# Weight block sums by accumulating DMAs in DRAM, and six of eight cms chunks multiplied down in pairs by seven products

## What is computed

```python
# L0, L2: V = 512, H = 2048
attn_out = softmax(q @ k.T * V**-0.5) @ v @ Wp + bp          # q, k, v = x @ Wq, x @ Wk, x @ Wv
cms_out  = gelu(attn_out @ cW1 + cb1) @ cW2 + cb2 + one_hot(target_codes)
modifier = gelu(concat([attn_out, cms_out]) @ mW1 + mb1) @ mW2 + mb2
x = clip(x + cms_out + modifier, 0, 1)
# L1, L3: 512 -> 256 -> 512, weights chosen by each batch's role
y = x + gelu(x @ W_down[role] + b_down) @ W_up[role] + b_up
x = layernorm(y) * gamma[role] + beta[role]
```

## Time and profile before

| | |
|---|---|
| median of 3 runs | 2156.77 us (2155.68 to 2158.98) |
| the profiled execution | 2156.44 us, span 2154.8 us |
| PE busy | 2105.6 us, 98%, 9256 matmuls |
| DVE / ACT / POOL busy | 1537.7 / 1042.1 / 598.7 us |
| DMA | 146.41 MB, 125767 packets |

### The profile page before, as it was taken

The page is one execution under the profiler, slowest core; times in us unless marked ns, Lnnn a source line. Parts: engine busy times, 40 slices in busy tenths (PEclk is TensorE's granted clock), DMA queues, the critical chain, the costliest instruction groups (busy, mean ns, idle before and its releaser), DMA issues.

```text
span 2154.8 us, 24846 instructions
## 1 busy us (share of the span) xinstructions
PE 2105.6 (98%) x9256; PEld 1724.7 (80%) x9256; DVE 1537.7 (71%) x1923; ACT 1042.1 (48%) x1527; POOL 598.7 (28%) x620
## 2 busy tenths in 40 slices
PE   8999999999999999999999999999999999999997
PEld 6888887888788887888877888788887888878884
DVE  4366678776867668876776766977686866787676
ACT  5264445454446444544554544444454644454444
POOL 1001136452001113655000111655400011355420
PEclk9999999999999999999999999999999999999999
DMA  8101131212202112221312111321130211311211
GB/s 304 40 10 59 59 88 49 59 48 78 100 20 88 59 59 69 59 59 59 116 41 88 40 59 42 96 59 59 40 127 20 102 46 59 88 50 59 59 59 39
DMA packets 125767, 146.41 MB, mean 68 GB/s; under 512 B 5952, under 2 KB 100160, under 8 KB 123728
## 3 DMA queue, kind: packets, MB, share of 16 engines
q1 hardware_dynamic: 122912, 130.05, 18.9%
q0 software_dynamic: 1504, 8.49, 1.9%
q10 hardware_dynamic: 1232, 6.29, 0.7%
HBM read 123.84 MB, written 12.58 MB: 63 GB/s over the span
## 4 chain that ended last, share of the span: by engine, by line
PE 85%; DVE 10%; ACT 2%; issue 2%; DMA 0%; SPq 0%; ACTq 0%; DVEq 0%
PE bank L615 28%; PE bank L617 28%; PE bank L616 28%; DVE ring L1321 2%; DVE vc L1363 2%; DVE pc L1493 1%; DVE xa L1358 1%; DVE lsum L1695 1%; ACT ring L955 1%; ACT raw L1098 0%; PE bank L923 0%; DVE xs L1700 0%; DVE xs L1653 0%; DVE xs L1685 0%; DVE raw L1439 0%
## 5 line engine op out<-in xcount | busy, mean ns | idle before, releaser
L1321 DVE TENSOR_TENSOR ring<-stage,ring 128x1024 fp32r<-128x1024 f32 (+1 forms) x312 | 363.4, 1176 | 103.8 <-ACT ring L955 103.6
L551 POOL TENSOR_TENSOR stage<-stage 128x256 f32<-128x256 f32 x120 | 106.3, 886 | 1122.1 <-DMA stage<-cms_w 904.5
L615 PE MATMUL bank<-ph_hi,ring 128*128 128x512 f32 x1048 | 410.6, 392 | 5.4 <-issue 2.4
L617 PE MATMUL bank<-ph_hi,ring 128*128 128x512 f32 x1048 | 407.9, 389 | 0.0
L616 PE MATMUL bank<-ph_lo,ring 128*128 128x512 f32 x1048 | 407.9, 389 | 0.0
L615 PE MATMUL bank<-xa,ring 128*128 128x512 f32 x1016 | 396.0, 390 | 2.9 <-DVE xs L1653 2.1
L617 PE MATMUL bank<-xa,ring 128*128 128x512 f32 x1016 | 395.3, 389 | 0.0
L616 PE MATMUL bank<-xa,ring 128*128 128x512 f32 x1016 | 395.3, 389 | 0.0
L955 ACT ACTIVATE ring<-stage 128x1024 fp32r<-128x1024 f32 (+1 forms) x312 | 296.3, 970 | 111.7 <-PE bank L617 78.3
L615 PEld LDWEIGHTS bank<-ph_hi,ring 128*128 128x128 f32 x1048 | 196.7, 188 | 53.7 <-issue 7.2
L617 PEld LDWEIGHTS bank<-ph_hi,ring 128*128 128x128 f32 x1048 | 196.7, 188 | 41.0
(11 more groups left out here) (159 smaller groups left out, 3139.6 us busy)
## 6 DMA issues: line engine op xcount, KB each, us to landing
stage<-mod_w SPq DMA_DIRECT2D x128, 256.0 KB, 3.4
stage<-cms_w SPq DMA_DIRECT2D x36, 512.0 KB, 3.6
stage<-mod_w SPq DMA_DIRECT2D x32, 512.0 KB, 4.9
stage<-cms_w SPq DMA_DIRECT2D x56, 256.0 KB, 4.3
fold_staging<-fold_w SPq DMA_DIRECT2D x16, 512.0 KB, 5.2
stage<-folded SPq DMA_DIRECT2D x16, 512.0 KB, 4.3
xs<-pc POOLq DMA_DIRECT2D x8, 1024.0 KB, 8.3
stage<-ada_w SPq DMA_DIRECT2D x16, 512.0 KB, 3.6
```

The source lines that it names most:

```text
L551: pool.tensor_tensor(part(S1), part(S2), part(A22), ALU.add).then_inc(sums_ready, 1)
L615: pe.matmul(dst, lh, rh, start=start and n == 0, stop=False, skip_group_check=not start)
L617: done = pe.matmul(dst, ll, rh, start=False, stop=n == last, skip_group_check=not start)
L1321: dve.tensor_tensor(ring_part(key, 1), staged(key), f32(ring_part(key, 0)), ALU.subtract).then_inc(w_lo, 1)
```

## The change

1. **Sums in DRAM.** New DRAM tensors `ready_w` and `ready_pair` hold each piece as seven blocks. SyncE copies the piece's blocks into them, seven DMAs a piece in DRAM (`prepare`); GpSimd adds with accumulating DMAs in rows of 8 KB, three once the copies are there (`sum_once`) and two once those are (`sum_twice`). Then `load_ready` brings all seven blocks to the staging buffer (896 KB, rows of 1 KB; 2 KB for a pair). The layer's 33 pieces (30, and three double ones) are cut in batches: for layer 0 one of three and one of five at the start, then two a slot in slots 0 to 7 and three from slot 8; for layer 1 two and four. Batch `n` is copied in SyncE's turn of slot `n + 1`, summed once in GpSimd's slot `n + 2` and twice in slot `n + 3`. Layer 0 is prepared in round 0, layer 1 in round 1. GpSimd's `sums` go.
2. **Pairs down.** Chunks 0 and 1, 2 and 3, 4 and 5 go down as pairs by seven products (`pair_product`, 12 matmuls each) and are added to `pc` by DVE (`pair_add`, 128x1024; for the first pair the four first ones are two tensor_scalars each). Chunks 6 and 7 stay plain. Fourteen hidden tiles a pair are split instead of eight, and eight hidden sums a pair are formed on GpSimd (`pair_sum`, 128x512), in free parts of `vc` and `ph`. A pair's weight (E, 14 blocks) lies over staging buffers 1 and 2; A has buffer 0 in all cms slots. Even and odd cms slots have lists of their own on PE, ACT and DVE; slot 7 is `cms_last`.

In `prepare`, kind D has four DMAs (seven blocks, runs of 1 KB). The core of the diff (in the parts on ACT, the lines of the old `slot` between them are left out):

```diff
+PAIR_PARTS = ((0, 2, 1), (6, 1, 1), (3, 2, 2), (2, 2, 2))
+PAIR_RING_GROUP = (4, 11, 14, 4)
...
+            def load_ready(key):
+                layer, at = key[0] // 2, STAGE_OF[key]
+                to = stage_pair if key[1] == "E" else stage[at]
+                n = READY_IN[layer, key[1:]]
+                sp.wait_ge(w_lo, STAGE_FREE[key])
+                sp.wait_ge(prepared[n], 16 * batch_count(layer, n, lambda kind: 2))
+                sp.dma_start(to[:, :, :], ready_piece(layer, *key[1:]).rearrange("b p n -> p b n")).then_inc(stage_in[at], 16)
+            def prepare(layer, slot):
+                under = ((A11, 0, 0), (A12, 0, 1), (S4, 0, 1), (S1, 1, 0), (S3, 1, 0), (S2, 1, 1), (A22, 1, 1))
+                for kind, n in BATCHES_READY[layer, slot]:
...
+                    elif kind == "E":
+                        chunks = cms_w[2 * (layer * CH + n - 1) + 1, :, :], piece
+                        for block, m, k in under:
+                            sp.dma_start(to[DOWN_AT[block], :, :].rearrange("p (k n) -> p k n", k=2),
+                                         chunks[k].rearrange("p (k m n) -> p k m n", k=2, m=2)[:, :, m, :]).then_inc(copied[slot], 16)
+                    else:
+                        halves = piece.rearrange("p (k m n) -> p k m n", k=4, m=2)
+                        for block, m, k in under:
+                            sp.dma_start(to[UP_AT[block], :, :].rearrange("p (k n) -> p k n", k=2),
+                                         halves[:, 2 * k:2 * k + 2, m, :]).then_inc(copied[slot], 16)
             def load_attend(r):
...
-            def sums(key):
-                s, done, at = stage[STAGE_OF[key]], SUM_AT[key], DOWN_AT if key[1] == "D" else UP_AT
-                def part(block):
-                    return s[:, at[block], :]
-                pool.wait_ge(stage_in[STAGE_OF[key]], 16 * STAGE_NTH[key])
-                pool.tensor_tensor(part(S1), part(S2), part(A22), ALU.add).then_inc(sums_ready, 1)
-                pool.tensor_tensor(part(S3), part(S2), part(A11), ALU.add).then_inc(sums_ready, 1)
-                pool.wait_ge(sums_ready, done + 2)
...
+            def rows(w, block):
+                return w[block, :, :].rearrange("(g q) n -> g (q n)", q=2048 // w.shape[2])
+            def sum_once(layer, slot):
+                pool.wait_ge(copied[slot], 16 * batch_count(layer, slot, COPIES.get))
+                for kind, n in BATCHES_READY[layer, slot]:
+                    w, at = ready_piece(layer, kind, n), UP_AT if kind in ("A", "C") else DOWN_AT
+                    for block, more in ((S1, A22), (S3, A11), (S4, A22)):
+                        pool.dma_start(rows(w, at[block]), rows(w, at[more]), accum_op=ALU.add, max_dma_last_dim=8192).then_inc(summed_once[slot], 16)
+            def sum_twice(layer, slot):
+                pool.wait_ge(summed_once[slot], 16 * batch_count(layer, slot, lambda kind: 3))
+                for kind, n in BATCHES_READY[layer, slot]:
+                    w, at = ready_piece(layer, kind, n), UP_AT if kind in ("A", "C") else DOWN_AT
+                    for block in (S2, S4):
+                        pool.dma_start(rows(w, at[block]), rows(w, at[S3]), accum_op=ALU.add, max_dma_last_dim=8192).then_inc(prepared[slot], 16)
+            def sum_ahead(r, n):
+                for step, before in ((sum_twice, 3), (sum_once, 2)):
+                    if n >= before and batch_in(r, n - before) is not None:
+                        step(batch_in(r, n - before), n - before)
...
+            def pair_product(r, i, q):
+                blk, at = OPERAND[q], RING_E[q] * BLK
+                pe.wait_ge(w_lo, W_AT[r, "E", 2 * i + 1, PAIR_GROUP[q]])
+                pe.wait_ge(h_lo, pair_split_at(r, i, blk, 1))
+                before = {Q6: Q1, Q7: Q6, Q4: Q7, Q3: Q5, Q2: Q3}
+                if q in before:
...
+            def pair_even(r, n):
+                i = n // 2 - 1
+                up(r, n, Q5)
+                up(r, n, Q1)
+                pair_product(r, i, Q3)
+                up(r, n, Q6)
+                up(r, n, Q2)
+                up(r, n, Q3)
+                up(r, n, Q7)
+                pair_product(r, i, Q6)
+                up(r, n, Q4)
+            def pair_odd(r, n):
+                i = n // 2
+                for q in UP_ORDER[up_order(n)][:2]:
+                    up(r, n, q)
+                if i:
+                    pair_product(r, i - 1, Q7)
+                up(r, n, Q6)
+                up(r, n, Q2)
+                if i:
+                    pair_product(r, i - 1, Q4)
+                up(r, n, Q3)
+                if i:
+                    pair_product(r, i - 1, Q2)
+                up(r, n, Q7)
+                pair_product(r, i, Q1)
+                up(r, n, Q4)
+                pair_product(r, i, Q5)
...
+            def pair_even(r, n):
+                i = n // 2 - 1
+                act.wait_ge(down_done, pair_down_at(r, i, Q5))
+                split_hi((r, "E", n - 1, 3))
+                split_hi((r, "A", n, 1))
                 take(r, n, Q1, bank[BANK[Q2]][:, :])
-                if not first:
-                    split_hi((r, "D", n - 1))
+                pair_t_hi(r, i, T3, 0)
+                pair_b_hi(r, i, B21, 1)
                 take(r, n, Q5, snap[:, 0, :])
+                pair_t_hi(r, i, T3, 1)
+                pair_t_hi(r, i, T4, 0)
                 take(r, n, Q6, bank[BANK[Q3]][:, :])
-                act.wait_ge(prod_done, prod_at(r, n, Q2))
-                act.wait_ge(h_lo, hidden_at(r, n - 1, 0))
...
+            def pair_odd(r, n):
+                i = n // 2
+                if i:
+                    split_hi((r, "A", n, 1))
+                if i == 0:
+                    split_hi((r, "E", n, 0))
+                    split_hi((r, "E", n, 1))
+                    act.wait_ge(gelu_done, gelu_at(r, 0, 3))
+                take(r, n, Q1, bank[BANK[Q2]][:, :])
+                if i:
+                    pair_b_hi(r, i, B11, 1)
+                take(r, n, Q5, snap[:, 0, :])
+                pair_t_hi(r, i, T1, 0)
+                pair_t_hi(r, i, T1, 1)
+                if i:
+                    act.wait_ge(down_done, pair_down_at(r, i - 1, Q7))
+                    split_hi((r, "E", n, 0))
+                    split_hi((r, "E", n, 1))
+                take(r, n, Q6, bank[BANK[Q3]][:, :])
+                up_turn(r, n, 0)
+                split_hi((r, "A", n + 1, 0))
+                up_turn(r, n, 2)
+                pair_b_hi(r, i, B22, 0)
+                if i:
+                    act.wait_ge(down_done, pair_down_at(r, i - 1, Q2))
+                pair_b_hi(r, i, B21, 0)
+                split_hi((r, "E", n, 2))
+                up_turn(r, n, 3)
+                pair_b_hi(r, i, B22, 1)
+                up_turn(r, n, 1)
...
+            def pair_even(r, n):
+                i = n // 2 - 1
+                pair_add(r, i, Q5)
+                split_lo((r, "E", n - 1, 3))
+                split_lo((r, "A", n, 1))
+                pair_split_lo(r, i, T3, 0)
+                pair_split_lo(r, i, B21, 1)
+                pair_split_lo(r, i, T2, 0)
+                pair_split_lo(r, i, T3, 1)
+                pair_add(r, i, Q3)
+                pair_split_lo(r, i, T2, 1)
+                combine(r, n, C12)
+                pair_split_lo(r, i, T4, 0)
+                combine(r, n, C22)
+                split_lo((r, "A", n + 1, 0))
+                pair_add(r, i, Q6)
...
+            def pair_odd(r, n):
+                i = n // 2
+                if i:
+                    split_lo((r, "A", n, 1))
+                    pair_split_lo(r, i, B11, 1)
+                    pair_add(r, i - 1, Q7)
+                pair_split_lo(r, i, T1, 0)
+                pair_split_lo(r, i, T1, 1)
+                split_lo((r, "E", n, 0))
+                split_lo((r, "E", n, 1))
+                split_lo((r, "A", n + 1, 0))
+                if i:
+                    pair_add(r, i - 1, Q4)
+                combine(r, n, C12)
+                combine(r, n, C22)
+                pair_split_lo(r, i, B22, 0)
+                if i:
+                    pair_add(r, i - 1, Q2)
+                pair_split_lo(r, i, B21, 0)
+                split_lo((r, "E", n, 2))
+                pair_add(r, i, Q1)
+                pair_split_lo(r, i, B22, 1)
```

More of the change, by code:

```diff
@@ L184, in weight_stream @@
         plain(r, "P", 0)
[L185 to L191 removed]
+        up(r, 1, 0)
+        ops.append((r, "A", 1, 1))
+        for n in range(1, CH - 1):
+            if n % 2 == 0:
+                ops.append((r, "E", n - 1, 3))
+            if n > 1:
+                ops.append((r, "A", n, 1))
+            if n % 2:
+                pair_first(r, n)
+                ops.append((r, "E", n, 1))
+            up(r, n + 1, 0)
+            if n % 2:
+                ops.append((r, "E", n, 2))
+        ops.append((r, "A", CH - 1, 1))
+        down(r, CH - 2)
+        staged_up(r, CH)
+        ops.append((r, "A", CH, 0))
+        down(r, CH - 1)
```

(25 more changed lines are left out.)

486 lines of the change are left out of this document (339 added, 147 removed).

## The result

The changed kernel takes 2232.5 us (median of 4 runs, 2228.3 to 2235.56), the kernel before 2157.88 us beside it: a ratio of 1.0345, 95% interval 1.0324 to 1.0365. It is 3.5% slower, where 2125 was forecast.

The account below looks back on a forecast made before the run. PE was taken as the bound, its time being its count of matmuls plus few gaps. The terms summed as 2156.4 - 32.6 - 7 + 4 + 5 = 2125.8, given as 2125 us, range 2113 to 2148.

Parts of the forecast that it names:

- Term 1: Cms chunks down on PE: pairing removes 144 matmuls (9256 to 9112), all on the path, saving 32.6 us.
- Terms 2 and 3: Pair slots: thin queue margins cost 4 us; end of cms stages: sums leaving POOL speed up DVE, saving 7 us.
- Term 4: Block sums by DMA in rounds 0 and 1: copies and accumulates mostly fit beside the loads, costing 5 us.
- Start: First early pieces of round 0: sums and load done by 98 us, ACT wants them at 138.68, cost 0.
- POOL's issues: GpSimd issuing additions in cms and modifier slots: ten take 5 to 9 us and fit, cost 0.
- the DMA engines become the bound: Rival in SP's queue, rounds 0 and 1: loads behind copies, from about 45 ns a packet; 2228 us at 53; chance 0.05.

Follow-up runs that it names:

- x1_no_prep: Changed kernel without copies or accumulates, its ready loads of the same size reading unsummed weights: 2120.55 us, ratio 0.9822 to the kernel before.
- x2_copies: Changed kernel with the copies kept but all accumulating transfers left out, loads waiting for the copies only: 2122.34 us, ratio 0.9831.
- x3_early: Changed kernel with the first two batches cut five and three pieces instead of three and five: 2215.88 us, ratio 1.0264.
- x14_plain: Changed kernel with GpSimd's accumulating transfers made plain, same bytes, waits and order, nothing added: 2155.48 us, ratio 0.9987.
- x11_loads_first: Changed kernel with SyncE issuing a slot's copies behind that slot's loads instead of ahead of them: 2218.76 us, ratio 1.0264.
- x10: Changed kernel with accumulating transfers in rows and packets of 2 KB in place of 8 KB: 2243.91 us, ratio 1.0393.

## Why the prediction was wrong, point by point

**Term 1** was right: 9112 matmuls, and from before to x1_no_prep PE's busy time falls by 32.2 us (2105.6 to 2073.4) against 32.6 forecast.

**Terms 2 and 3** forecast +4 and -7. PE's idle time falls from 49.2 to 45.6 us in x1_no_prep, 3.6 against 3 in sum. The sum is met, the two terms are not measured apart. What is seen of them: in round 2 of the changed kernel the pair slots keep up (DVE 81%, not 76%; its splits of a pair's weight take 1655 ns each where 1222 was taken); the row that took 2.746 us takes 1.226, as forecast, and the gap of 1.52 us is 0.82, not gone:

```profile
L2047 DVE SCALAR_TENSOR_TENSOR raw<-raw,pc 128x1024 f32<-128x1024 f32 x4 | 4.9, 1226 | 0.1
```
```profile
1460.64 0.50 PE L831 MATMUL bank<-vc,ring 128*128 128x512 f32 x1 [0.82 <-DVE ring L1674]
```

**Term 4 is the step that failed:** +5 was taken, 112 came (2120.55 to 2232.5). Its prices for a copy and an addition were good, its use of them was not, and a slot's loads were set too low.
- A copy's packet: x2_copies has 112,448 packets more than x1_no_prep on SP's queue and 3631 us of engines more (37.1% of 16 x 2119.6 less 26.4% of 16 x 2119.0), 32 ns each on average; 35 was taken.
```profile
q1 hardware_dynamic: 247520, 252.75, 37.1%
```
```profile
q1 hardware_dynamic: 135072, 186.66, 26.4%
```
- An addition of 128 KB: 83 us a MB x 0.131 / 16 = 0.68 us; 0.63 was taken, from the residuals, which add too. So the factor of two was in the price already.
- With 35 ns I had 17 us for a slot of 19, 27 for 28.5 and, in four slots, 33 for 28.5, and then called the rest "a slot's slack". Four slots over by 4.5 us are 18 us by my own numbers, not 5. And the count was of pieces: a pair piece has twice the bytes, so a batch with one is three units. Such a slot of round 1 asks for 21 copies x 0.45 (3631/16/504), 15 additions x 0.68 and, with the pair's load, 7.8 us: 27 us for 19. There the gaps are largest (12.04 and 13.36), and round 0, with no such batch after the early ones, has 6.80 and 7.77.
- The loads: in x1_no_prep a packet of 1 KB of a ready load took 52 ns and one of 2 KB of a pair's 87, so the 896 packets of each are 2.9 and 4.9 us of all 16 engines. With a pair every second slot that is 5.4 us a slot; 3.0 to 4.5 was taken.
- So an ordinary slot of two pieces asks for 14 x 0.45 + 10 x 0.68 + 5.4 = 18.5 us of 19. That is full, not a slot with slack: a load must land in the 6 to 10 us before its split, and in those it meets 14 copies and the additions at once.

**Start: cost 0 forecast, 15.56 us found.** The load of the first up piece was reckoned at 98 us; SP's queue comes to it only when the split of P frees the stage, near 111 us, the second early batch is copied behind it, and POOL's additions of that batch stand ahead of T1. I had followed the load through SP's queue and not the next batch through POOL's. x3_early gives half of it back.

**What enters no sum:** the clock. I held 1.00 because PE stays dense. It did not: PE's busy time is 27.5 us longer than in x1_no_prep for the same 9112 matmuls (2100.9 less 2073.4), a quarter of the loss.

**POOL's issues** were priced right. In a burst of ten they start 0.50 us apart and the last ends 7.9 us after the first starts, 0.79 us each, though DVE is busy; 5 to 9 us was forecast:

```profile
260.55 3.14 POOL L735 DMA_DIRECT2D ready_w<-ready_w  x4
262.58 5.84 POOL L727 DMA_DIRECT2D ready_w<-ready_w  x6
```

The Trainium skill's figure of 3.1 us for such an issue ("SBUF — State Buffer", the note on DVE blocking DMA) is not seen here: its case is a DVE copy, and DVE's rows in these slots are mostly additions and subtractions of two tensors. The page of the profile does give 3165 ns as the mean row of line L727, but that is queueing within a burst: the first row of this burst takes 0.77 us and each next one some 0.29 us more. Without the addition (x14_plain) the rows do not lengthen, and an issue takes 0.48 us. What the forecast left out is what stands behind a burst: the two sums T1 at 172.71 us, right behind ten issues, took 5.38 us together.

**The rival** "the DMA engines become the bound" said 2228 and had 0.05. Its sign came true (rounds 0 and 1 longer, PE waiting for a split that waits for a stage load). Its bound was right, and its time by luck, as its price of 53 ns a packet was not met (32). Its place and its threshold were wrong: copies alone, in that place, cost 1.8 us (x2_copies), and moving them out of it gives back 14 (x11_loads_first). At 32 ns, below its 45, the bound was reached all the same, by the additions and the pair pieces.

What stays open: how the 33 us of plain transfers and the 77 of additions divide between bursts over the engines, latency in the chain copy, first sums, second sums, load, and POOL's longer issues. In x14_plain, gaps of 7.36 and 5.84 us remain in the cms stage of round 1.

## What to carry to other kernels

Work moved from an idle-looking engine to the DMA engines must be summed per slot, in bytes, with its largest pieces and with the loads that have to land in the same microseconds; a mean share of 0.7 over a stage can hide stretches at 1.0. Price it from the queue rows of the profile, an accumulating transfer at twice a plain one, count a piece of twice the size as two, and do not read a sum of nine tenths of the slot as "fits": here it stood for a slot that was full by the measured prices. Of the complete versions tried, only one was faster than the kernel before: it moves the cms pieces alone, spread one to a slot, and leaves the other sums where they were.

## What the runs showed of the hardware

- An accumulating transfer within DRAM holds the DMA engines 83 us of one engine a MB, the same transfer without addition 44.
- Copies within DRAM cost 32 ns a packet on average, less than the 53 ns that the queue's mean had suggested: in x2_copies a packet of 512 B took 28 ns and one of 1 KB 52 ns.
- Neighbouring rows of a DRAM to DRAM transfer are joined into packets up to the given limit: asking for rows of 2 KB alone changed no packet (261418 both times), with the limit at 2048 there are 278698.
- With packets of 2 KB POOL's issues of additions come to a stop for up to 9.2 us at a time (x10: 45 times, 195 us in all); with 8 KB no such stop is seen in the changed kernel.
- POOL needs 0.79 us for the issue of an accumulating transfer and 0.48 for the same one without addition (bursts of ten; changed kernel and x14_plain).
- SP's issue of the same 14 copies took 12.59 us without additions beside it and 16.24 with them.
- Long gaps of PE are paid twice, by a fall to the 1.2 GHz level that outlasts them (granted clock 0.69 from 229 to 240 us, behind the gap of 6.80): 85 us more idle time than in x1_no_prep came with 27.5 us more busy time for the same matmuls.
